# First stage of a vision-tower kernel: GpSimd's sum of two products made in two halves, each with its own signal

## What is computed

```
h = s4d_kernel(log_dt, x, B, inv_A_real, A_imag, 1024)        # 64 channels, 128 rows, length 1024
h = h + attention(layernorm(h), wq, wk, wv, wo)
h = h + lora_ffn(layernorm(h), W_base, b_base, lora_A, lora_B, router_W, router_b, ...)
```

```
A  = -exp(inv_A_real) + 1j * A_imag;   dtA = A * exp(log_dt)[:, None]
C' = B * (x[..., 0] + 1j * x[..., 1]) * (exp(dtA) - 1) / A
K  = 2 * einsum('chn,hnl->chl', C', exp(dtA[:, :, None] * arange(1024))).real
```

## Time and profile before

| | |
|---|---|
| median of 3 runs | 3069.84 us (3069.07 to 3070.4) |
| the profiled execution | 3072.73 us |
| its span, from first to last instruction | 3070.9 us |
| TensorE busy in the span | 2848.9 us (93%) |
| VectorE busy | 2452.0 us (80%) |
| first stage | the first 245.7 us of the span |

### The profile page before, as it was taken

How to read it: one execution, slowest core, us unless ns; L and a number is a source line. 1 busy time by engine, 2 the same in 40 slices (tenths; PEclk the granted TensorE clock), 3 DMA queues, 4 the chain that set the end, 5 groups by cost and what they waited for, 6 DMA issues and landing times.

```text
span 3070.9 us, 61939 instructions
## 1 busy us (share of the span) xinstructions
PE 2848.9 (93%) x16986; PEld 1413.5 (46%) x16986; DVE 2452.0 (80%) x8675; ACT 1899.1 (62%) x5933; POOL 1965.6 (64%) x1722
## 2 busy tenths in 40 slices
PE   4777579999999999999999999999999999999986
PEld 3655234444444444444444444444444444444432
DVE  7886468888888888888888888888888888888872
ACT  5774366566666666666666666666666666666651
POOL 2440167677766777777667776766677677677762
PEclk9887789999999999999999999999999999999988
DMA  6875276766676666666666666666666666666751
GB/s 182 205 195 131 55 138 148 140 148 145 147 148 149 148 145 146 146 145 146 151 148 144 147 145 149 145 151 144 146 145 148 148 143 151 146 149 143 144 119 52
DMA packets 1252624, 442.59 MB, mean 144 GB/s; under 512 B 1200049, under 2 KB 1208497, under 8 KB 1252417
## 3 DMA queue, kind: packets, MB, share of 16 engines
q1 hardware_dynamic: 1252416, 440.69, 65.2%
HBM read 88.22 MB, written 67.11 MB: 51 GB/s over the span
## 4 chain that ended last, share of the span: by engine, by line
PE 29%; DVE 21%; issue 16%; POOL 13%; ACT 8%; DMA 2%; DVEq 1%; ACTq 0%; POOLq 0%; SPq 0%
PE bank_b L1446 14%; PE bank_a L1446 11%; DVE heads L1267 6%; ACT probs L1088 6%; DVE probs L1213 6%; POOL p_hl L1013 4%; POOL probs L1009 4%; POOL rope_a L1019 2%; DVE share L1222 2%; POOL xy_hl L1028 2%; PE score L1417 1%; DVE r L1295 1%; DVE r L1302 1%; DVE zs L1375 1%; PE pv L1435 1%
## 5 line engine op out<-in xcount | busy, mean ns | idle before, releaser
L1088 ACT ACTIVATE probs<-probs,negmax 128x128 f32<-128x128 f32 x2048 | 789.7, 387 | 265.7 <-DVE negmax L1213 265.7
L1013 POOL TENSOR_TENSOR p_hl<-probs,p_hl 128x512 f16<-128x512 f32 x512 | 615.2, 1202 | 346.9 <-ACT p_hl L1097 344.8
L1009 POOL TENSOR_TENSOR probs<-probs,rsum 128x512 f32<-128x512 f32 x512 | 556.7, 1087 | 219.0 <-DVE rsum L1224 217.8
L1446 PE MATMUL bank_a<-qkv_hi,xt 128*128 128x512 f16 x2048 | 656.4, 382 | 28.9 <-DMA xt<-xy_hl 28.9
L1446 PE MATMUL bank_b<-b_hi,yt 128*128 128x512 f16 x2048 | 644.5, 381 | 0.0
L1213 DVE CUSTOM_DVE_ANT_0 probs<-score,table,scal 128x128 f32<-128x128 f32 x2048 | 596.2, 347 | 49.3 <-issue 48.6
L1097 ACT ACTIVATE p_hl<-probs 128x512 f16<-128x512 f32 x512 | 319.9, 625 | 427.0 <-POOL probs L1009 419.3
L1267 DVE TENSOR_TENSOR heads<-rope_a,heads 128x512 f16<-128x512 f32 x320 | 397.7, 1258 | 36.4 <-ACT heads L1118 36.4
L1446 PE MATMUL bank_a<-qkv_lo,xt 128*128 128x512 f16 x1024 | 391.2, 382 | 0.0
L1446 PE MATMUL bank_b<-b_lo,yt 128*128 128x512 f16 x1024 | 390.8, 382 | 0.0
L1446 PE MATMUL bank_b<-o_hi,at_lo 128*128 128x512 f16 x1024 | 388.9, 380 | 0.0
(11 more groups left out here) (201 smaller groups left out, 4458.6 us busy)
## 6 DMA issues: line engine op xcount, KB each, us to landing
tok_h<-kout SPq DMA_DIRECT2D x64, 512.0 KB, 5.5
hin<-tok_h SPq DMA_DIRECT2D x64, 512.0 KB, 3.3
r<-tok_h SPq DMA_DIRECT2D x64, 512.0 KB, 3.6
out_dram<-r SPq DMA_DIRECT2D x64, 512.0 KB, 2.9
probs_t<-p_hl SPq DMA_TRANSPOSE x512, 2.8
xc<-in_x_dram SPq DMA_DIRECT2D x32, 128.0 KB, 4.2
raw_a<-in_L_attn_wq_dram SPq DMA_DIRECT2D x1, 4096.0 KB, 13.8
raw_b<-in_L_attn_wo_dram SPq DMA_DIRECT2D x32, 128.0 KB, 3.7
```

Of the source, the lines that this page charges most:

```text
L1009: TT(x, x, rsum[:, u % 4].unsqueeze(2).to_broadcast([P, GR, T]), ALU.mult).then_inc(s_norm, 1)
L1013: TT(p_hl[:, u % 2, 1], probs[:, u % 4], p_hl[:, u % 2, 0], ALU.subtract).then_inc(s_plo, 1)
L1088: ins = A(probs[:, u % 4, g], probs[:, u % 4, g], ACT.Exp, bias=negmax[:, u % 4, g:g + 1], scale=-1.0, accum_out=sums[:, u % 4, g:g + 1])
L1446: ins = MM(bank, x(c), w[:, c, cols], start=(c == 0 and i == 0), stop=(c == KC - 1 and i == 2))
```

## The change

In POOL's body the one addition over 8 rows becomes two additions over 4 rows each, and each one signals `s_z`. `s_z` therefore counts two for a chunk, and both engines that wait for it count so: DVE waits for both halves of the chunk whose buffer it overwrites, and PE waits for the first half before row 0 and for the second before row 4.

```
-                    nc.gpsimd.tensor_tensor(z[:, r], z[:, r], z2[:, r], ALU.add).then_inc(s_z, 1)
+                    for i in range(2):
+                        half = slice(CH // 2 * i, CH // 2 * (i + 1))
+                        nc.gpsimd.tensor_tensor(z[:, r, half], z[:, r, half], z2[:, r, half], ALU.add).then_inc(s_z, 1)
...
-                        dve.wait_ge(s_z, ch)
+                        dve.wait_ge(s_z, ch * 2)
...
-                pe.wait_ge(s_z, ch + 1)
                 pe.wait_ge(s_v, ch + 1)
                 for h in range(CH):
+                    if h % 4 == 0:
+                        pe.wait_ge(s_z, ch * 2 + (h // 4 + 1))
```

## The result

The changed kernel takes 3053.91 us in the median of five runs (3050.03 to 3055.67), the kernel before beside it 3070.40 (3069.07 to 3070.82): a ratio of 0.9946, 95% interval 0.9932 to 0.9961. That is 16.5 us faster; 3053.6 was forecast. A second session gave 3052.38, ratio 0.9944. The profiled execution took 3050.03 with a span of 3048.2, so it is the fastest of the five, 3.9 under the median.

A forecast was written before the change was run, and what follows sets the result against it. It took the chunk-pair loop, with DVE waiting for TensorE's rows, as the bound: 21.0 (waits) - 1.8 (L408) - 6 (clock) + 3 (tail) = 16.2 us gained, from 3069.84 to 3053.6, range 3046 to 3062.5.

The forecast's parts named there:

- What bounds: First stage, pair of chunks as a loop: DVE's L428 waits for TensorE's rows seven times, 21.0 us to win.
- The halves: POOL's addition: each half takes 2.3 us, both 4.6; the extra is 0.06 a chunk, 1 us in all without idle cover.
- The start: PE's row 0 of the even chunk: can start at T + 2.5 in place of T + 4.8, 2.26 us earlier.
- T: The time at which DVE's L420 of the even chunk ends, 142.34 in the pair examined.
- The clock, the term of 6: PE's bursts: six tenths of 14 lose the clock, each making DVE wait 0.7, costing 6 us; bounds 0 and 10.5.
- the spare of 1.5: Even chunk at full clock: PE's last row done at T + 9.8, DVE ready at T + 11.3, 1.5 us to spare.
- warm throughout: Rival on PE's bursts: none loses the clock, 23.2 us gained, 3046.6 us; chance 0.22.
- What VectorE pays, the term of 1.8: DVE's L408 runs beside POOL's swap in odd chunks too: 0.3 for six chunks, 1.8 us; bounds 0 and 3.6.
- The tail: End of the first stage, copies waiting for stores: moves earlier with the last even burst, 2.26 to 4, taken as 3 us.
- The sum: Whole kernel: 21.0 - 1.8 - 6 + 3 = 16.2 us gained, giving 3053.6 us; forecast chance 0.52.
- Transfers: Rival: DMA, 21.0 us a pair against DVE's 22.7, becomes the bound; needing a tenth more, gain 8, 3062; chance 0.10.

The follow-up runs named there:

- e1: Changed kernel, but TensorE waits for both halves of the addition before row 0: 3072.64 us, ratio 1.0006 to the kernel before.
- e9: Changed kernel with the addition in four quarters of two rows, TensorE waiting before every second row: 3051.33 us, ratio 0.9938 to the kernel before.
- e4: Changed kernel with four extra matmuls on constants in every chunk from the second on: 3044.39 us, ratio 0.9916 to the kernel before.
- e7: Changed kernel with VectorE's weight reduction over an eighth of each slice, leaving out seven eighths: 3046.85 us, ratio 0.9924 to the kernel before.
- e5: Kernel before with extra matmuls on constants, nine in even and six in odd chunks from the second on: 3053.00 us, ratio 0.9942.
- e3: Kernel before with nine extra matmuls on constants in even chunks only: 3063.77 us, ratio 0.9976.
- e11: Changed kernel with GpSimd's swap ahead of the waits and addition, plus four matmuls on constants a chunk: 3048.83 us, ratio 0.9932 to the kernel before.
- e10: Changed kernel with GpSimd's swap ahead of the waits and the addition: 3054.37 us, ratio 0.9947 to the kernel before.

## Why the prediction was right, step by step

- **What bounds.** Right. The wait of L428 was the sum to win, and it went from 21.0 to 1.4; e1 shows that it comes back with the late signal. VectorE comes next, as the forecast said: e9 has no wait left and is no faster.
- **The halves.** 2.357 us each for 2.3; they cost 2.4 of GpSimd's busy time in the stage for 1.0. In e1, where nothing is won, the stage ends 1.8 later.
- **The start.** T + 2.6 in place of T + 2.5 (110.74 to 113.38).
- **The clock, the term of 6.** Mis-sized, at most 1.9. A burst that lost the clock took 8.86 for 7.17 in nearly every case, so 1.7 for the 2.2 taken over from the kernel before, where the long gaps cost up to 3.0. With the spare of 1.5 that leaves waits of 0.16 to 0.56, not 0.7. Holding the clock in every burst (e4) won just 1.6 to 1.9. It was also lost less often: in six of the last fourteen bursts (five in the second trace), where the forecast had 8.4. The rival "warm throughout" did not come about: gaps of 2.17 to 3.4 lost the clock in places. But the stage is near that case, since the loss was nearly all spare. The Trainium skill, "TensorE: Matmul & The Clock Gate", section "Why this matters for your kernels", would have had a gap as short as the 2.64 us before 67.45 keep the clock; that burst lost it and the one behind 3.62 us did not, and the rows decide.
- **What VectorE pays, the term of 1.8.** Mis-sized too, on the other side: 3.1. L408 took 0.6 of it in total; the rest is the small copy (L405, now L407), which took 5.6 in all for 3.1. The forecast looked at L408 alone. Where L430 starts a little after L422 ends, as at 110.85 (the burst before it, which lost the clock, ended at 110.81), the copy stands beside the swap and takes up to 0.66 for 0.19, and L410 is free of it; where L430 follows at once, as at 122.32, L410 takes 1.56 and the copy 0.27.
- **The tail.** 2.7 for 3: from the last L430 (202.98) to the next stage 23.6 us; in the kernel before it was 26.3, from this row to 245.7:

```profile
219.44 2.28 DVE L428 TENSOR_TENSOR z<-ct,tabc 128x2048 f32<-128x2048 f32 x1
```

- **The sum.** 21.0 - 3.1 - 1.4 + 2.7 = 19.2, which is the 19.1 seen in the stage, and not 16.2. The median gained 16.5 and 18.6 in two sessions. The part after the stage takes up to 7 us more or less from kernel to kernel with no edit in it, so the closeness of 3053.91 to 3053.6 is partly luck: the forecast of the stage was 3 short.
- **Transfers.** The DMA share rose from 0.83 to 0.91 between 60 and 222 us. VectorE was busy 140.1 of the 142 us from 60 to 202 all the same, so they bound nothing there; in e7, with a shorter loop, ACT waited for stores 16 us.
- **A point that was not seen.** The forecast treats the clock as an addition to the earlier start. By e5, holding the clock in the kernel before is worth 14.3 of the 19.1 by itself, and e3 shows that holding it in half of the chunks is worth 2.0: in both kernels the clock was lost behind the longer of the two gaps of a pair, and filling one gap lengthened the other. The two gains overlap: with the clock held, the earlier start adds 6.4 (e5 to e4), not 19.1.

## What to carry to other kernels

Price a signal that comes earlier by the wait that closes the loop, here 21.0 us on VectorE, not by the idle time of the engine that is signalled, which was 48.7 and is still 31.7 to 40. When the loop's wait is gone, more pieces only add their cost (quarters: 5 us of GpSimd work and 4 us of VectorE work, nothing won). Before counting a lost clock as time, look for how much spare stands behind the burst; and where an engine shared with another becomes the bound, list every instruction that will now run beside it, small copies too.

## What the runs showed of the hardware

- Whether TensorE loses its clock is not a matter of the gap's length alone: after 3.62 us idle the burst at 125.04 kept 2.4 GHz (7.17), after 3.38 the one at 101.95 lost it (8.86), and after 2.64 the one at 67.45 lost it too. In e11 it was lost after 1.94.

```profile
67.45 8.86 PE L484 MATMUL kps<-v,z 128*128 128x256 f32 x32 [2.64 <-POOL z L255]
```

- Four matmuls a chunk on constants, 1.9 us of work on an idle engine, held 2.4 GHz from 60 to 222 us (1.00 for 0.94) and left VectorE's busy time unchanged (148.84 for 149.19). In e11 the same four did not always suffice (0.99 over the same stretch, one burst of 8.86).

```profile
60.00:222.00 162.00, 140.29 (x672) 117.85 (x672) 148.84 (x120) 134.18 (x250) 78.46 (x51) 1.00 0.94 225
...
60.00:222.00 162.00, 125.13 (x560) 104.89 (x560) 149.19 (x120) 135.29 (x247) 78.32 (x51) 0.94 0.91 223
```

  The first line is of the filled kernel, the second of the changed one.
- VectorE's products out of PSUM (L430, L431) took 2.28 beside GpSimd's addition as without it (L430 at 31.5, before GpSimd's first addition at 41.9: all sixteen between 2.28 and 2.29). Beside GpSimd's swap a copy of 80 elements took up to 0.66 for 0.19, and products of two SBUF operands 1.56 for 1.23 (L410), 1.43 for 1.22 and 1.64 for 1.28 (L424 and L425 of e10).
